# Spreading the later layers of a graph network over 39 slots, with shared roots and a longer product lag

## The reference

```python
# L0: an MLP on every pair (i, j), normalized, then weighted by adj
h = relu((x @ W1[:128])[:, :, None, :] + (x @ W1[128:])[:, None, :, :] + b1)   # 128x128 pairs x 128
y = layernorm(einsum('bijk,kl->bijl', h, W2) + b2) * gamma + beta
x = layernorm(x + einsum('bij,bijh->bih', adj, y))
# L1: d = rowsum(adj) ** -0.5 (0 where the sum is 0); relu((adj * d_i * d_j) @ x @ W.T + b)
x = layernorm(x + L1)
# L2: ((1 + eps) * x + adj.T @ x) @ W1 -> relu -> @ W2, masked
x = layernorm(x + L2)
# L3: three times h = relu(layernorm(adj.T @ (h @ W) + b + h) * gamma + beta)
x = layernorm(x + L3)
```

## Time and profile before

| | |
|---|---|
| median of 3 runs | 2755.82 us (2755.48 to 2756.5) |
| the profiled execution | 2755.1 us, its span 2753.5 us |
| TensorE busy, matmuls | 2690.3 us (98%) |
| VectorE, ScalarE, GpSimd busy | 95%, 93%, 90% |
| granted TensorE clock over the span | 0.989 |
| HBM | 205 GB/s over the span |

### The profile page before, as it was taken

The page is one execution under the profiler, slowest core; times in us unless marked ns, Lnnn a source line. Parts: engine busy times, 40 slices in busy tenths (PEclk is TensorE's granted clock), DMA queues, the critical chain, the costliest instruction groups (busy, mean ns, idle before and its releaser), DMA issues.

```text
span 2753.5 us, 60836 instructions
## 1 busy us (share of the span) xinstructions
PE 2690.3 (98%) x10882; PEld 1147.3 (42%) x10882; DVE 2619.0 (95%) x20102; ACT 2567.7 (93%) x6903; POOL 2487.8 (90%) x3498
## 2 busy tenths in 40 slices
PE   8999999999999999999999999999999999999993
PEld 2344444444444444444444444444444444444442
DVE  4999999999999999999999999999999999999997
ACT  7999999999999999999999999999999999999991
POOL 3899999999999999999999999999999999999992
PEclk9999999999999999999999999999999999999995
DMA  3655655655555555556556555555655565565562
GB/s 108 237 196 209 231 206 196 231 219 194 215 231 201 202 226 219 197 215 231 199 200 232 214 194 221 227 199 203 230 213 197 214 236 196 202 234 210 195 228 95
DMA packets 188668, 571.72 MB, mean 208 GB/s; under 512 B 70656, under 2 KB 106368, under 8 KB 139136
## 3 DMA queue, kind: packets, MB, share of 16 engines
q1 hardware_dynamic: 188288, 567.83, 54.5%
HBM read 555.17 MB, written 8.39 MB: 205 GB/s over the span
## 4 chain that ended last, share of the span: by engine, by line
PE 67%; ACT 18%; DVE 8%; issue 6%; POOL 1%; DMA 0%; SPq 0%; ACTq 0%; DVEq 0%; POOLq 0%
PE y_ps L417 47%; PE ss_ps L429 13%; ACT h L556 11%; DVE h L685 5%; ACT sq L566 4%; ACT dev_rows L573 2%; PE prod_bank L479 1%; PE prod_bank L483 1%; PE prod_bank L450 1%; ACT hid L595 1%; PE prod_bank L456 1%; PE prod_bank L457 1%; PE uv_ps L402 1%; PE uv_ps L403 1%; POOL h L924 1%
## 5 line engine op out<-in xcount | busy, mean ns | idle before, releaser
L924 POOL TENSOR_SCALAR h<-vT,uT 128x128 f32<-128x128 f32 x2520 | 2056.7, 831 | 23.7 <-ACT vT L546 23.3
L417 PE MATMUL y_ps<-h,w2c 128*128 128x512 f32 x4096 | 2016.4, 609 | 11.4 <-DVE h L669 1.6
L685 DVE CUSTOM_DVE_ANT_0 h<-h,cb 128x128 f32<-128x128 f32 x8192 | 1983.9, 289 | 10.0 <-DVE gT_keep L749 0.5
L556 ACT ACTIVATE h<-uv_ps,uT 128x128 f32<-128x128 f32 x4848 | 1409.2, 433 | 0.0
L566 ACT ACTIVATE sq<-y_ps,b2c_col 128x1024 f32<-128x1024 f32 x1024 | 1182.5, 1155 | 112.3 <-PE y_ps L417 112.1
L417 PEld LDWEIGHTS y_ps<-h,w2c 128*128 128x128 f32 x4096 | 682.2, 190 | 903.6 <-issue 723.7
L685 DVE DVE_READ_ACCUMULATOR2_ANT gT<- 128x1 f32 x8192 | 636.8, 78 | 0.1
L429 PE MATMUL ss_ps<-sq,sel 128*32 128x512 f32 x4096 | 545.5, 605 | 0.9 <-ACT sq L566 0.9
L915 POOL TENSOR_TENSOR rs<-var_eps,minus_half 128x1 f32<-128x1 f32 x448 | 302.7, 676 | 35.1
L669 DVE TENSOR_SCALAR h<-vT,uT 128x128 f32<-128x128 f32 x757 | 200.9, 294 | 4.7 <-ACT mask_all L611 2.6
L912 POOL TENSOR_TENSOR var_eps<-mv,eps_col 128x1 f32<-128x1 f32 x448 | 96.1, 215 | 117.9 <-DVE mv L712 115.0
(11 more groups left out here) (100 smaller groups left out, 1489.8 us busy)
## 6 DMA issues: line engine op xcount, KB each, us to landing
cb<-c_scratch SPq DMA_DIRECT2D x384, 1024.0 KB, 9.3
cb<-c_scratch SPq DMA_DIRECT2D x256, 512.0 KB, 4.8
adj_c<-in_adj_dram SPq DMA_DIRECT2D x512, 8.0 KB
devs<-dev_rows SPq DMA_DIRECT2D x512, 8.0 KB
x_in<-in_x_dram SPq DMA_DIRECT2D x64, 64.0 KB, 10.8
c_scratch<-c SPq DMA_DIRECT2D x128, 32.0 KB, 1.5
adj_in<-in_adj_dram SPq DMA_DIRECT2D x64, 64.0 KB, 4.4
x_res<-in_x_dram SPq DMA_DIRECT2D x64, 64.0 KB, 5.4
```

What stands on the lines that cost most here:

```text
L417: op = pe.matmul(y_ps[:, t % 2, c0:c0 + COLS], w2c[:], h[:, (SLOTS * g + t) % H_RING, c0:c0 + COLS], start=True, stop=True)
L556: op = act.activation(h[:, (SLOTS * g + t) % H_RING, n * P:(n + 1) * P], v, ACT.Relu, bias=uT[:, b, i:i + 1])
L685: op = dve.tensor_tensor_reduce(h[:, (SLOTS * g + t) % H_RING, cols], h[:, (SLOTS * g + t) % H_RING, cols], cb[:, t // 2, c0:c0 + P], 1.0, ...
L924: op = pool.tensor_scalar(h[:, (SLOTS * g + t) % H_RING, n * P:(n + 1) * P], vT[:, b, :], uT[:, b, i:i + 1], 0.0, ALU.add, ALU.max)
```

## The change

- Lags: products 6 slots after the start (was 5), squares 7, variances 8 (still in groups of two slots), deviations 15, coefficients 18, weighted sums 21. The rings of `h` and `sq` grow to 20 and 6 slots.
- Units: a table per slot for VectorE (9 a graph, was 11) and GpSimd (40); ScalarE makes 79. In the last two slots of a graph (was one) it reads v from SBUF.
- The later layers have new places up to slot 38, so a third older graph is in flight (`tails` over 2, 3, 4), with one more draining iteration.
- Roots: `pair_of_roots` takes a norm of one graph and one of the graph before in one power of two columns; `last_roots` does so for the degree and the last norm. The last graph takes its roots on ScalarE (Sqrt) and VectorE (reciprocal).
- The row sums of the coefficients are paired by small DMAs, so `c_sum_mm` and `rows_sum` are gone; `gT` has two buffers and no copy.
- The spread coefficients have a ring of six chunks, not eight. `unit_of` is in order, `load_adj_c_rows` is two DMAs. `load_tail` stands after `straighten_deviations`.
- Start: the weights w1, w2 and the rest have semaphores of their own; part of the set-up stands in slots (`first_set_up`, `later_set_up_done`).

```diff
-TTR_LAG = START + 15
-H_RING = 18
+PRODUCT_LAG = START + 2
+SQUARE_LAG = PRODUCT_LAG + 1
+VARIANCE_LAG = PRODUCT_LAG + 2
+DEVIATION_LAG = PRODUCT_LAG + 9
+COEFFICIENT_LAG = DEVIATION_LAG + 3
+TTR_LAG = START + 17
+H_RING = 20
 LAYERS = 3
-SQ_RING = 4
-ROOTLESS = (1, 2, 3, 5, 7, 9, 11, 14)
+SQ_RING = 6
+GROUP = 2
+VECTOR_UNITS = (1, 1, 1, 1, 2, 1, 0, 0, 0, 0, 0, 0, 1, 0, 1, 0)
+POOL_UNITS = (3, 3, 1, 1, 3, 3, 3, 1, 3, 3, 3, 3, 3, 3, 2, 2)
 SPAN = P // 2
-WEIGHTS = 7
+FIRST_WEIGHTS = 3
+WEIGHTS = 3
 LATER_WEIGHTS = 8 + 4 * LAYERS
 PARTS = 3
 CHUNKS = HALF // 2
+CB_RING = 6
...
-    if g == 0 or t == SLOTS - 1:
-        return BLOCK_UNITS
-    return t % 2
+    return BLOCK_UNITS if g == 0 else VECTOR_UNITS[t]
...
-    return 3 if (t + START) % SLOTS in ROOTLESS else 2
+    return POOL_UNITS[t]
...
-    ("adj_turn", 0, 0), ("adj_turned", 0, 6), ("row_sum", 0, 2), ("degree", 0, 5), ("has_degree", 1, 5),
-    ("c_sum_mm", 1, 4), ("c_sum", 1, 8), ("x_base", 2, 3),
-    ("g_keep", 3, 4), ("l0_mm", 4, 0), ("l0_sum", 4, 5), ("ln0", 4, 6), ("x1_scaled", 5, 6),
-    ("l1_agg", 6, 0), ("l1_agg_keep", 6, 8), ("l1_mm", 7, 0), ("l1_bias", 7, 7), ("l1_relu", 8, 0),
-    ("ln1", 8, 2), ("l2_agg", 9, 4), ("l2_agg_keep", 10, 2),
-    ("l2_mm1", 10, 4), ("l2_relu", 11, 2), ("l2_mm2", 11, 4), ("l2_sum", 12, 2), ("ln2", 12, 3),
-    ("l3_agg0", 13, 4), ("l3_agg_keep0", 14, 2), ("l3_mm0", 14, 4), ("l3_sum0", 15, 2),
-    ("l3_ln0", 15, 3), ("l3_relu0", 17, 2), ("l3_agg1", 20, 0), ("l3_agg_keep1", 20, 8),
-    ("l3_mm1", 21, 0), ("l3_sum1", 22, 1), ("l3_ln1", 22, 2), ("l3_relu1", 23, 6),
-    ("l3_agg2", 24, 0), ("l3_agg_keep2", 24, 8), ("l3_mm2", 25, 0), ("l3_sum2", 26, 1), ("l3_ln2", 26, 2),
-    ("l3_relu2", 27, 6), ("final_sum", 29, 2), ("ln3", 29, 3),
+    ("make_uv", 2, 4), ("c_sum", 3, 3), ("keep_uv", 3, 5), ("adj_turn", 3, 5), ("row_sum", 4, 4), ("degree", 4, 7),
+    ("adj_turned", 5, 1), ("x_base", 6, 6), ("l0_mm", 6, 6), ("l0_sum", 7, 2), ("ln0", 7, 5), ("roots0", 7, 8),
+    ("ln0_norm", 8, 8), ("has_degree", 9, 0), ("x1_scaled", 9, 6), ("l1_agg", 10, 5), ("l1_agg_keep", 10, 6),
+    ("l1_mm", 11, 7), ("l1_bias", 12, 1), ("l1_relu", 12, 7), ("ln1", 13, 1), ("roots1", 13, 2), ("turn_x", 13, 4),
+    ("ln1_norm", 13, 8), ("l2_agg", 14, 5), ("keep_x", 15, 3), ("l2_agg_keep", 15, 5), ("l2_mm1", 16, 1),
+    ("l2_relu", 16, 1), ("l2_mm2", 16, 4), ("roots2", 17, 7), ("l2_sum", 18, 3), ("ln2", 18, 8), ("l3_agg0", 19, 6),
+    ("ln2_norm", 20, 0), ("l3_agg_keep0", 20, 1), ("l3_mm0", 21, 2), ("l3_sum0", 21, 6), ("l3_ln0", 23, 5),
+    ("l3_ln0_norm", 24, 8), ("l3_relu0", 26, 0), ("l3_agg1", 26, 5), ("l3_agg_keep1", 26, 5), ("l3_mm1", 27, 5),
+    ("l3_sum1", 28, 6), ("l3_ln1", 29, 0), ("l3_ln1_norm", 30, 1), ("l3_relu1", 30, 7), ("l3_agg2", 32, 8),
+    ("l3_agg_keep2", 32, 8), ("l3_mm2", 33, 8), ("l3_sum2", 34, 5), ("l3_ln2", 35, 1), ("l3_relu2", 35, 8),
+    ("l3_ln2_norm", 36, 2), ("final_sum", 36, 5), ("roots_last", 36, 6), ("ln3", 37, 3), ("ln3_norm", 38, 4),
...
+            def pair_row_sums(g, b, half):
+
+                wait_apart(sp, c_made, 2 * g + half + 1)
+                wait_apart(sp, c_sum_set, g - 1)
+                wait_apart(sp, c_pair_in[half], 32 * g)
+                for l in range(2):
+                    sp.dma_start(c_pair[SPAN * half:SPAN * half + SPAN, b, l:l + 1], c_row_sum[l:P:2, half:half + 1]
+                                 ).then_inc(c_pair_in[half], 16)
+
             def spread_coefficients(g, half):
 
                 wait_apart(sp, c_stored[half], 16 * (g + 1))
                 for p in range(CHUNKS):
-                    wait_apart(sp, ttr_done, SLOTS * (g - 1) + HALF * half + 2 * p + 2)
+                    k = 2 * CHUNKS * g + CHUNKS * half + p
+                    wait_apart(sp, ttr_done, 2 * (k - CB_RING) + 2)
...
-                new, old, older, oldest = graphs
+                new, old, oldest = graphs[0], graphs[1], graphs[4]
                 if old is not None:
                     spread_coefficients(old, 0)
+                    pair_row_sums(old, 1 - buf, 0)
                 if after is not None:
                     wait_apart(sp, x_turned, new + 1)
                     wait_apart(sp, x_in_in, 16 * (new + 1))
...
                     spread_coefficients(old, 1)
                     if new is not None:
                         load_adj_c(new)
-                    load_tail(old, 1 - buf)
+                    pair_row_sums(old, 1 - buf, 1)
                 if new is not None:
                     straighten_deviations(new, 0)
+                if old is not None:
+                    load_tail(old, 1 - buf)
                 if oldest is not None:
                     wait_apart(sp, normed["ln3"], oldest + 1)
                     wait_apart(sp, out_stored, 16 * oldest)
-                    sp.dma_start(out[oldest], x4[:, 1 - buf, :]).then_inc(out_stored, 16)
+                    sp.dma_start(out[oldest], x4[:, buf, :]).then_inc(out_stored, 16)
...
-                if due("c_sum_mm"):
-                    wait(pe, rows_kept, g + 1)
+                if due("l0_mm"):
                     wait(pe, adjT_set, g + 1)
-                    for half in range(2):
-                        op = pe.matmul(c_sum_ps[b], row_pick[:, half, :], rows_sum[:, half:half + 1],
-                                       start=(half == 0), stop=(half == 1))
-                    op.then_inc(c_summed, 1)
-                if due("l0_mm"):
-                    wait(pe, c_sum_set, g + 1)
-                    wait(pe, g_kept, g + 1)
-                    pe.matmul(out, gT_keep[:, b, :], w2cg[:], start=True, stop=False)
+                    wait(pe, ttr_done, SLOTS * (g + 1))
+                    pe.matmul(out, gT[:, b, :], w2cg[:], start=True, stop=False)
...
+            def later_set_up_done():
+
                 pe.wait_ge(wT_set, 1)
                 pe.wait_ge(mask_set, 1)
                 pe.wait_ge(pick_set, PARTS)
                 pe.wait_ge(bias_set, PARTS)
                 pe.wait_ge(eps_set, 2)
-                pe.wait_ge(row_pick_set, 3)
+                pe.wait_ge(affine_set, 2)
...
-            pe.wait_ge(weights_in, 16 * WEIGHTS)
-            pe.wait_ge(w2c_set, 1)
-            pe.wait_ge(affine_set, 2)
+            pe.wait_ge(w1_in, 16 * FIRST_WEIGHTS)
             pe.wait_ge(ones_set, 3)
             pe.wait_ge(set_up, 1)
 
...
                 for s in range(SLOTS):
                     if is_graph(new, 1) and s == LATER_SET_UP_SLOT:
                         later_set_up()
-                    yg, t = lagging(graphs, s, START + 1)
+                    if is_graph(new, 1) and s == LATER_SET_UP_SLOT + 2:
+                        later_set_up_done()
+                    yg, t = lagging(graphs, s, PRODUCT_LAG)
                     if yg is not None:
                         products(yg, t, 0)
-                    if s == START - 1 and new is not None:
-                        make_uv(new)
+                    own_steps(after, new, buf, s * FINE, s * FINE + 4)
...
+                for name in NORMS:
+                    if g == G - 1 and lo <= AT[name] + 2 < hi:
+                        wait(act, mv_set[name], g + 1)
+                        act.activation(var_eps[:, b:b + 1], mv[:, b, 1:2], ACT.Sqrt, bias=EPS).then_inc(dev_set[name], 1)
...
+            def wait_root(g, name):
+
+                if g == G - 1:
+                    wait(dve, rs_set[name], 1)
+                elif name == "ln3":
+                    wait(dve, last_rooted, g + 3)
+                for i, (first, second) in enumerate(PAIRS):
+                    if g < G - 1 and name == first:
+                        wait(dve, pair_rooted[i], g + 1)
+                    if g < G - 1 and name == second:
+                        wait(dve, pair_rooted[i], g + 2)
...
-                if lo <= AT["degree"] < hi:
-                    wait(pool, degree_floor_set, g + 1)
-                    wait(pool, dis_set, g - 1)
-                    pool.tensor_tensor(dis_raw[:, b:b + 1], degree_floor[:, b:b + 1], minus_half[:], ALU.pow
-                                       ).then_inc(dis_raw_set, 1)
-                for name in NORMS:
-                    if lo <= AT[name] + 1 < hi:
-                        wait(pool, mv_set[name], g + 1)
-                        pool.tensor_tensor(var_eps[:, b:b + 1], mv[:, b, 1:2], eps_col[:], ALU.add
-                                           ).then_inc(eps_added[name], 1)
-                        wait(pool, eps_added[name], g + 1)
-                        pool.tensor_tensor(rs[:, b:b + 1], var_eps[:, b:b + 1], minus_half[:], ALU.pow
-                                           ).then_inc(rs_set[name], 1)
+                for i, (first, second) in enumerate(PAIRS):
+                    if lo <= AT[f"roots{i}"] < hi:
+                        pair_of_roots(g, b, i, first, second)
+                if g < 2 and lo <= AT["roots_last"] - 2 * SLOTS * FINE < hi:
+                    last_roots(g, None, b)
```

(81 more changed lines are left out.)

190 lines of the change are left out of this document (100 added, 90 removed).

## The result

| | before | after |
|---|---|---|
| median (range) | 2756.16 us (2755.48 to 2756.66) | 2777.51 us (2776.32 to 2777.53) |
| ratio, 95% interval | | 1.0077 (1.0059 to 1.0094) |
| profiled execution, its span | 2755.1, 2753.5 us | 2777.5, 2775.7 us |

The forecast was 2716 us (2706 to 2744): wrong in sign.

The account below looks back on a forecast made before the run. TensorE, busy 41.74 of 41.85 us a graph, was taken as the bound. From 2755.1 us, - 21 - 16.5 + 3 - 4 - 1.5 + 0 gave 2715.1, forecast as a 2716 us median; range 2706 to 2744.

Parts of the forecast that it names:

- (e): Later layers' order: same TensorE cost over 39 slots, not 30; closest places l2_mm2 behind l2_relu, l3_agg0 behind ln2_norm.
- (f): New waits from the two closest later-layer places: 0.05 us a graph, +3 us; bounds 0 and +0.5 us a graph.
- (c): ScalarE makes 79 units, not 77: its need rises 0.9 us to 41.0 of 41.25 us, just under TensorE.
- (a): c_sum_mm leaves TensorE's full list: 0.34 us a graph over 62 graphs, -21 us.
- (b): Products lag two slots, not one, so TensorE's 0.27 us wait for hidden units goes: -16.5 us, bounds 0 to -16.5.
- (d): VectorE falls about 1.0 us to 39.6; GpSimd loses 3.3 us, ending between 35.8 and 37.6, two-column power taken as free.
- The start: Products start at 8.2 us, not 12.17, with no wait for gamma: -4 us, bounds -3 and -4.5.
- The set-up and the first three graphs: Graph 1's waits for the set-up stand two slots later: -1.5 us, range 0 to -2.2.
- The drain: At the end: weighted sums +1.9 us, later steps about 1, norms -2.8, gT copy -0.3; sum 0, bounds -5 and +5.
- A: The wait moves instead of going: TensorE waits 0.2 to 0.5 us a graph, 2725 to 2744 us; chance 0.27.
- B: load_tail meets a spread of coefficients and adj_turn holds TensorE 3 to 4 us a graph: 2930 us; chance 0.10.
- C: Six chunks: late VectorE sums delay l0_mm by 0.5 us a graph, about 2750 us; chance 0.05.

Follow-up runs that it names:

- e10: e4 with START at 5 and PRODUCT_LAG at 6, so hidden units come one slot before their products again: 2841.52 us, ratio 1.031.
- e4: The changed kernel with l3_agg_keep2 moved to (33, 1), l2_mm2 to (17, 1) and l3_agg_keep1 to (27, 1): 2715.93 us, ratio 0.9852.
- e3: The changed kernel with l3_agg_keep2 moved from (32, 8) to (33, 1) and l2_mm2 from (16, 4) to (17, 1): 2728.01 us, ratio 0.9896.
- e2: The changed kernel with only l2_mm2 on TensorE moved from (16, 4) to (17, 1): 2730.92 us, ratio 0.9905.

## Why the prediction was wrong

**The step that failed is (e) with its price (f).** It charged 0.05 us a graph for new waits, at most 0.5; measured are 0.63 + 0.48 = 1.11. Three errors are in it.
- Only TensorE's consumers were gone through. The diff shows `l3_agg1` and `l3_agg_keep1` both at (26, 5) and `l3_agg2` and `l3_agg_keep2` both at (32, 8), where before each copy stood eight fine places behind. That the copies would hold ScalarE, 2.15 us a graph, was never asked. "The others have more than 1 us" covers TensorE's later-layer matmuls, of which indeed no other waits; the variances, which wait 0.48 us for squares of a late ScalarE, were not among them.
- `l2_mm2` behind `l2_relu` was named as the closest place and even given overlapping times (needed 1.9 us into the slot, ready at 1.6 to 2.0), and still priced at nearly nothing. And the relu's length before was no guide: its mean was 0.36 us there and is 0.69 after, as its row is drawn out (last section):

```profile
L595 ACT ACTIVATE hid<-prod_bank,l2b 128x128 f32<-128x128 f32 x64 | 23.0, 359 | 1.8 <-PE prod_bank L471 1.8
L642 ACT ACTIVATE hid<-prod_bank,l2b 128x128 f32<-128x128 f32 x64 | 44.0, 688 | 1.8 <-PE prod_bank L499 1.8
```

- The margins were taken one by one with everything else in time. In a loop each wait makes the next one.

Term (c) had ScalarE at 41.0 of 41.25 us. That was busy time with its drawn-out ends; by steps its list is 39.5 us, so it had some 1.8 us of room. It was not too full: its room stood in the wrong places.

**What was right.** (a): 0.34 us forecast, 0.35 by the lists. (b): the product stands 0.05 us behind each bias matmul, the old wait never shows; e10, which brings such waits back, moves more than the lag, so that the longer lag removed it is supported and not isolated. (c): the steps of units are 0.25 us from PSUM and 0.292 from SBUF, so ten more of the latter are +0.42, against +0.4.

**What was off without harm.** (d): VectorE fell to 40.10, not 39.6. GpSimd fell by 1.4 us to 37.70, not by 3.3 to 35.8, and just outside the bound of 37.6. Its 40 units are part of that: they take 856 ns where they took 831, 1.0 us a graph, which no term had and whose cause is open. The two-column power is another; it costs neither nothing nor 0.46 us more:

```profile
L1008 POOL TENSOR_SCALAR h<-vT,uT 128x128 f32<-128x128 f32 x2520 | 2113.5, 856 | 25.5 <-ACT vT L587 25.2 <-DVE gT L730 0.3
L981 POOL TENSOR_TENSOR rs<-var_eps,minus_half 128x2 f32<-128x2 f32 (+1 forms) x192 | 160.9, 838 | 15.1
```

838 ns against 676 is +0.16. By the rule of the Trainium skill (GPSIMD Engine Reference, 3.1) it would be near 0; the trace decides for 0.16, and in the steady graphs TensorE has no other waits than the two in the table. The start gave 4.6 us against 4. The set-up and the first three graphs gave 2.2, less than the 1.5 plus three graphs' gain. The drain cost 2.2 us against 0, within its bounds. In the last norms the roots on ScalarE answer to the earlier trace rows; `x` starts 0.82 us after the start of the variance's row, and VectorE no longer idles 1.00 us there (timeline of after, all engines):

```profile
2743.97 0.30 DVE L757 BATCH_NORM_AGGREGATE mv<-stats 128x2 f32<-128x6 f32 x2
2744.17 0.20 ACT L627 ACTIVATE var_eps<-mv 128x1 f32<-128x1 f32 x1 [4.98 <-DVE mv L757]
...
2744.61 0.15 DVE L760 RECIPROCAL rs<-var_eps 128x1 f32<-128x1 f32 x1
...
2744.79 0.34 DVE L783 TENSOR_SCALAR x<-z,mv,rs 128x128 f32<-128x128 f32 x1
```

**The rivals.** A was the mechanism, with the wait put at 0.2 to 0.5 us where it is 1.1; its far end, 2744, is 33.5 us short. B did not come, and its row says so against the earlier trace rows: adj_in lands 1.8 us after its issue in the median and 2.5 at most, and no matmul waits for it. C did not come: VectorE waited for cb 2.7 us in the whole run, once.

```profile
adj_in<-in_adj_dram SPq DMA_DIRECT2D x64, 64.0 KB, 1.8
```

With three places moved (e4) the change measures 2715.93 us at a period of 41.33; the forecast was 2716 at 41.3. TensorE's terms of work were right, the order was not.

## What to carry to other kernels

Where every engine runs a fixed list, go through the diff of the order once per engine, not only for the one that bounds: a consumer that is placed level with its producer can be a wait that everything behind it inherits, even on an engine whose own list is 1.8 us shorter than the bounding one. It need not be: `l2_mm1` and `l2_relu` both stand at (16, 1), and ScalarE waits for that matmul only twice in the whole run. If a margin comes out as "ready at 1.6 to 2.0, needed at 1.9", price it with both engines late, as a loop, and let the range reach there. Follow the waits from one to the next until the way comes back to its start: a wait that is not on it is worth nothing (e3 against e2). Take ScalarE's waits from steps between starts, since a drawn-out row can hide half a microsecond of idle time.
